# A pass over all tokens ahead of the mixer: LayerNorm, the dt path and the split of h move out of its half-steps, the decay masks become one fp32 operand, and TensorE takes a chunk's exponents at the end of a half-step

## The reference

```python
h = layernorm(x) * (1 + scale) + shift            # per batch b
zxbcdt = h @ W_in                                  # z 512, xBC 768, dt 8 heads
dt = softplus(dt + dt_bias);  A = -exp(A_log)
xBC = silu(conv4(xBC) + conv_b)                    # causal, 4 taps, per channel
h_t = h_{t-1} * exp(dt*A) + dt * x_t (x) B_t;  y_t = C_t . h_t + D*x_t
y = rms(y * silu(z)) @ W_out;  y = y + h
y = y + a * sigmoid(gate);  (a, gate) = y @ glu_w + glu_b
x2 = x + sign/size gate * layernorm(y)
out = x2 + gate * experts(layernorm(x2))           # 16 experts, top 4, and a shared one
```

## Time and profile before

| | us |
|---|---|
| median of 3 runs (2523.81 to 2525.84) | 2524.52 |
| the profiled execution | 2520.89 |
| its span | 2518.0 |
| first matmul of the mixer's xbc projection | 61.12 |
| first and last `add_h` (32 of them) | 115.0, 1267.6 |
| first load of the expert stage | 1285.7 |
| busy: PE, DVE, ACT, POOL | 2236.5, 1914.6, 1199.9, 854.9 |
| DMA queue of SP, share of its 16 engines | 7.5% |

### The profile page before, as it was taken

How to read it: one execution, slowest core, us unless ns; L and a number is a source line. 1 busy time by engine, 2 the same in 40 slices (tenths; PEclk the granted TensorE clock), 3 DMA queues, 4 the chain that set the end, 5 groups by cost and what they waited for, 6 DMA issues and landing times. The chain is left out here.

```text
span 2518.0 us, 43347 instructions
## 1 busy us (share of the span) xinstructions
PE 2236.5 (89%) x13488; PEld 1939.3 (77%) x13488; DVE 1914.6 (76%) x4376; ACT 1199.9 (48%) x2443; POOL 854.9 (34%) x729
## 2 busy tenths in 40 slices
PE   2788888888888888888759999999999999999998
PEld 2677777777777777777648888888888888888887
DVE  3799998899998899898847666766666665666755
ACT  1666766766766666676624333323333323333322
POOL 0233333333333333233323333333333333333333
PEclk7899999999999999999969999999999999999999
DMA  2000000000000000000031000000000000000000
GB/s 93 5 26 17 21 25 25 12 25 25 12 25 25 12 25 25 12 25 21 14 97 49 26 26 27 26 18 9 26 27 26 27 17 10 26 26 27 18 18 9
DMA packets 36586, 63.36 MB, mean 25 GB/s; under 512 B 4320, under 2 KB 13024, under 8 KB 36320
## 3 DMA queue, kind: packets, MB, share of 16 engines
q1 hardware_dynamic: 36448, 61.59, 7.5%
HBM read 44.80 MB, written 16.78 MB: 24 GB/s over the span
## 5 line engine op out<-in xcount | busy, mean ns | idle before, releaser
L1673 POOL TENSOR_TENSOR fl<-ff,fh 128x512 fp32r<-128x512 f32 x272 | 353.0, 1298 | 761.2 <-ACT fh L1467 761.2
L1586 DVE TENSOR_TENSOR ff<-gs,bank 128x512 f32<-128x512 f32 x272 | 186.8, 687 | 380.0 <-ACT gs L1461 326.3
L104 PE MATMUL bank<-mhh,wh 128*128 128x512 f32 x1088 | 435.9, 401 | 9.7 <-issue 9.7
L105 PE MATMUL bank<-mhl,wh 128*128 128x512 f32 x1088 | 431.0, 396 | 0.0
L106 PE MATMUL bank<-mhh,wl 128*128 128x512 f32 x1088 | 430.4, 396 | 0.0
L1608 DVE SCALAR_TENSOR_TENSOR acc<-bank,comb,acc 128x256 f32<-128x256 f32 x960 | 398.0, 477 | 8.9
L1467 ACT ACTIVATE fh<-ff 128x512 fp32r<-128x512 f32 x272 | 172.1, 633 | 447.4 <-DVE ff L1586 414.1
L1461 ACT ACTIVATE gs<-bank 128x512 f32<-128x512 f32 x272 | 162.5, 598 | 368.4 <-PE bank L106 368.4
L875 DVE SCALAR_TENSOR_TENSOR cv<-xc,convw,cv 128x256 f32<-128x256 f32 x576 | 321.2, 624 | 1.9 <-ACT cv L701 1.9
L104 PE MATMUL bank<-wh,fh 128*128 128x256 f32 x1088 | 306.9, 282 | 3.6 <-issue 1.6
L106 PE MATMUL bank<-wh,fl 128*128 128x256 f32 x1088 | 305.6, 281 | 0.0
(11 more groups left out here) (185 smaller groups left out, 5009.4 us busy)
## 6 DMA issues: line engine op xcount, KB each, us to landing
xt<-in_x SPq DMA_DIRECT2D x32, 256.0 KB, 2.7
xr<-in_x SPq DMA_DIRECT2D x32, 256.0 KB, 2.6
x_dram<-xr SPq DMA_DIRECT2D x32, 256.0 KB, 2.0
x<-x_dram SPq DMA_DIRECT2D x16, 512.0 KB, 3.6
xres<-x_dram SPq DMA_DIRECT2D x16, 512.0 KB, 4.5
out<-yo SPq DMA_DIRECT2D x16, 512.0 KB, 3.2
raw<-in_experts SPq DMA_DIRECT2D x17, 384.0 KB, 3.2
wmod<-in_wmod SPq DMA_DIRECT2D x1, 1536.0 KB, 6.4
```

Of the source, the lines that this page charges most:

```text
L104: pe.matmul(out, a_hi, b_hi, start=start, stop=False, skip_group_check=True)
L105: pe.matmul(out, a_hi, b_lo, start=False, stop=False, skip_group_check=True)
L1586: dve.tensor_tensor(ff[e % 2][:, :], g, UP[e % 2][:, :], ALU.mult).then_inc(ff_done, 1)
L1673: pool.tensor_tensor(fl[e % 2][:, :], ff[e % 2][:, :], fh[e % 2][:, :].bitcast(F32), ALU.subtract).then_inc(fl_done, 1)
```

## The change

A new function `prepare_tokens` runs ahead of the mixer, over all 8192 tokens in 16 groups of 512. It loads x, takes mean and variance, applies them, transposes, modulates twice from PSUM (hT and hh), subtracts (hl), projects dt into one PSUM bank for all tokens, and stores hT, hh and hl to DRAM. Then softplus runs once on 128x512 values, the three sums follow, and five parameters for each token and head (dt, a, and three exponentials or products) go to DRAM as `par_dram`. The splits of the weights, which stood in a block of their own, run in the same pass. The mixer's half-steps load hTh, hTl, hT and the parameters (`load_halves`, `load_h`, `load_par`) and lose the work listed above.

The decay masks are one fp32 operand: `mask_a` on DVE writes it, and `exponents` multiplies it by the fp32 matrix `after` with one matmul for four heads where there were two fp32r ones. In PE's list `exponents` of chunk 0 moves to the end of the half-step before.

```diff
+    x = [sb(f"px{n}", [P, MT, D]) for n in range(XBUF)]        # XBUF = 4
+    hT = two("phT", ...); hh = two("phh", ..., F32R); hl = two("phl", ..., F32R)
+        def load(n):
+            if n >= XBUF:
+                sp.wait_ge(xnT_ps, KD * (n - XBUF + 1))
+            sp.dma_start(x[n % XBUF]..., rows(t["x"], n)...)
+        def store(n):
+            for done, dst, src in ((hT_done, h_dram[0], hT), (hh_done, h_dram[1], hh), (hl_done, h_dram[2], hl)):
+                sp.wait_ge(done, ...)
+                sp.dma_start(rows(dst, n).rearrange("s p k t -> p k s t"), src[n % 2]...).then_inc(stored[n % 2], 16)
...
+        def modulate(n):
+            if n >= 2:
+                act.wait_ge(stored[n % 2], 48 * (n // 2))
...
+        pe.wait_ge(c_in, CONSTS)
+        turn(0)
+        for n in range(GROUPS):
+            if n + 1 < GROUPS:
+                turn(n + 1)
+            project_dt(n)
+        pe.wait_ge(a_done, 1)
+        for n, m in enumerate((upto, after, ones)):
+            pe.matmul(SUMS[n][:, :], m[:, :], a[:, :], start=True, stop=True).then_inc(sums_ps, 1)
...
 def exponents(b, i, c):
-    pe.wait_ge(au_done[b], CH * i + c + 1)
-    pe.wait_ge(lo_done[b], CH * i + c + 1)
+    pe.wait_ge(mask_done[b], CH * i + c + 1)
     if c == 0:
         pe.wait_ge(xc_done[b], 3 * i + 3)
         pe.wait_ge(tap0_done[b], 3 * i + 3)
-        pe.wait_ge(ex_done[b], i + 1)
+        pe.wait_ge(st_done[b], CH * i)
...
-        pe.matmul(Q(b, 2 + half_heads)[:, :], after_r[:, :], masked_hi[b]..., start=True, stop=False)
-        last = pe.matmul(Q(b, 2 + half_heads)[:, :], after_r[:, :], masked_lo[b]..., start=False, stop=True)
+        last = pe.matmul(Q(b, 2 + half_heads)[:, :], after[:, :], masked[b]..., start=True, stop=True)
...
 # PE's half-step
     if tail:
         project_out(*tail)
     if second:
-        exponents(*second, 0)
-    if first:
-        transpose_xn(*first)
-    if second:
         x_by_token(*second, 0)
         x_by_token(*second, 1)
     if tail:
         state_add(*tail, 1)
         glu(*tail)
-    if first:
-        project_dt(*first)
     if second:
         exponents(*second, 1)
...
     if first:
         project_z(*first, 0)
-        sums(*first)
     if second:
         transpose_y(*second, 1)
+    if first:
+        exponents(*first, 0)
...
 # DVE's half-step
+    if second:
+        mask_a(*second, 1)
     if tail:
         add_h(*tail)
...
-        mask_a_lo(*first, 0)
+        mask_a(*first, 0)
```

More of the change, by code:

```diff
@@ L203, in mixer @@
+def mixer(nc, sem, prime, t, mod, gate_ln, ident, minus_half, bank, h_dram, par_dram, x2_dram):
     with ExitStack() as ctx:
@@ L253, in mixer @@
         btok = both("btok", [P, CH, NS])
[L254 to L257, removed]
+        masked = both("masked", [P, CH, H, P])
         dec = both("dec", [P, CH, H, P])
@@ L456, in half @@
                     if more:
-                        load_x(*following(second))
+                        load_halves(*following(second))
+                    if first:
+                        load_par(*first)
+                        load_h(*first)
                     if tail:
@@ L511, in project_z @@
                     last.then_inc(z_ps[b], 1)
-                def sums(b, i):
-                    pe.wait_ge(a_done[b], i + 1)
-                    a = dts[b][:, 7, :, :]
-                    for n, m in enumerate((upto, after, ones)):
-                        last = pe.matmul(Q(b, 3)[:, 64 + n * CH * H:64 + (n + 1) * CH * H], m[:, :],
-                                         a.rearrange("p c h -> p (c h)"), start=True, stop=True)
-                    last.then_inc(sums_ps[b], 1)
                 def x_by_token(b, i, c):
@@ L552, in exponents @@
                         heads = slice(half_heads * 4, half_heads * 4 + 4)
-                        pe.matmul(Q(b, 2 + half_heads)[:, :], after_r[:, :],
-                                  masked_hi[b][:, c, heads, :].rearrange("p h i -> p (h i)"), start=True, stop=False)
-                        last = pe.matmul(Q(b, 2 + half_heads)[:, :], after_r[:, :],
-                                         masked_lo[b][:, heads, :].rearrange("p h i -> p (h i)"),
-                                         start=False, stop=True)
+                        last = pe.matmul(Q(b, 2 + half_heads)[:, :], after[:, :],
+                                         masked[b][:, c, heads, :].rearrange("p h i -> p (h i)"),
+                                         start=True, stop=True)
                     last.then_inc(dec_ps[b], 1)
@@ L1055, in half @@
                     if second:
-                        mask_a_lo(*second, 1)
-                    if more:
-                        norm1(*following(second))
-                    if second:
                         for c in range(CH):
@@ L1062, in half @@
                             times_end(*second, c)
-                    if first:
-                        softplus_head(*first)
                     if tail:
                         gated(*tail)
-                    if first:
-                        for step in range(5):
-                            softplus_step(*first, step)
                     if second:
@@ L1101, in half @@
                         mean_square(*second, 1)
-                    if first:
-                        for step in range(11, DT_LINKS):
-                            softplus_step(*first, step)
-                    if second:
                         split_yT(*second, 0)
                     if first:
-                        split_a(*first)
-                        mask_a_lo(*first, 0)
+                        mask_a(*first, 0)
                     if second:
                         split_yT(*second, 1)
-                    if more:
-                        apply1(*following(second))
                     if first:
                         conv(*first, 1)
-                for b in range(NB):
-                    norm1(b, 1)
-                    apply1(b, 1)
                 halves(dve, half)
@@ L1182, in half @@
                         split_y1(*tail)
-                    if first:
-                        split_h(*first)
                     if second:
@@ L1193, in half @@
                         root_y(*second, 1)
-                    if more:
-                        root_norm1(*following(second))
-                for b in range(NB):
-                    root_norm1(b, 1)
                 halves(pool, half)
```

533 lines of the change are left out of this document (281 added, 252 removed).

## The result

The median went from 2524.16 us to 2595.1 us: a ratio of 1.0281 [1.0263, 1.0299], slower by 71 us. The forecast was 2608, with 2555 to 2660 around it. The profiled execution took 2593.5 us.

What follows compares the result with a forecast made beforehand. The mixer was taken as bound by a chain through all engines, with waits and low clock on PE. First pass +119, first half-steps -7, half-steps -28: +84 us, a median of 2608, range 2555 to 2660.

Steps and rivals of the forecast that it cites:

- The pass: Ahead of the mixer: 16 groups at 6.5 us plus an uncovered tail, first xbc matmul at 180, +119 us.
- P: The mixer's half-step, from one add_h to the next: 37.18 us before, forecast 36.3, a gain of 28 us over 31.
- The row of waits in the half-step: PE's half-step walked from o, the end of project_out: waits of 1.7 us before the GLU, 1.9 before chunk-0 exponents.
- The half-step's low clock: PE in the mixer: a low stretch of 1.5 us in some three of four half-steps, +1.1 us on each half-step.
- the walk without it: Mixer half-step on PE at full clock, from one end of project_out to the next: 35.2 us.
- the engines need less: In the first pass: PE 5.3 us a group, below the 6.5 us of loads and stores.
- the 302 of the earlier trace: First pass's stores: 1 KB runs go at 302 GB/s with DMA engines full, 5.2 us a group.
- The rival in which the pass overlaps at full rate: First pass: 1 KB stores at 416 GB/s, so engines' 5.4 us a group decide; -22 us, 2586; chance 0.13.
- The prologue: First half-steps, with no norm, dt and mask chain ahead of them: 7 us shorter.
- DVE as the bound: Mixer: DVE sets the period, half-step 29.7 us, -120 us in all, 2405; chance 0.11.
- the decision point named for that rival: Mixer half-step below 33.6 us, where DVE setting the period would be decided.
- The rival in which the clock falls more often: Mixer: a further 1.5 us low stretch in each half-step, 37.5 to 37.8 us, total 2645; chance 0.16.

Runs made afterwards that it cites:

- experiment 3: Kernel before with fp32 masks written by DVE, and the next chunk 0's exponents at the end of the half-step: 2605.54 us, 1.0331 to the kernel before.
- experiment 1: Changed kernel with only the exponents of chunk 0 put back behind project_out: 2481.0 us, 0.9823 to the kernel before.
- experiments 2: Kernel before with the fp32 masks on DVE and one fp32 matmul for four heads, all else as before: 2423.94 us, 0.9603.
- experiment 4: Kernel before with the fp32 masks, plus sixteen ACT activations a half-step into a tile nobody reads: 2511.86 us, 0.9956 to the kernel before.
- experiment 9: Changed kernel without the h_t store and with POOL's root of group n+2 ahead of the subtraction of group n: 2580.75 us, 1.0237.

## Why the prediction held, and where it was off

**The direction and the mechanism were right.** The pass costs more than the half-steps give back. By the experiments, one edit on top of the other, from the kernel before: the masks alone -101 us (P -3.07), the moved work on top of them +57 (+129 for the pass, P -2.20, which is -68), the exponents at the end +114 (P +3.62). Each price holds where it stands in that row: put straight on the masks, the exponents at the end cost 182 us (experiment 3), and the moved work on top of both gives some 10 back. The row of waits in the half-step was met nearly to the tenth: the GLU at o + 3.4 behind 1.49 us of waiting (walked 3.4 and 1.7), chunk 1's exponents at 7.57 (7.65), `from_state` at 12.67 (12.75), pair 1 of xbc at 20.7 (20.85), the second transpose of y at 26.5 (26.85), the chunk-0 exponents at 28.95 behind 1.80 (29.15 and 1.9), released by `start_conv` as named.

**The number is nearer than its terms.** The half-steps gave 23 us more than forecast and the first matmul came 10.5 later; that 84 us of span were forecast and 73.7 measured is in part luck, as the two misses went opposite ways.

**The half-step's low clock was mis-sized.** P came out at 35.53 for 36.3. The term was +1.1 for a low stretch of 1.5 us in three of four half-steps; the walk without it gave 35.2. From one `add_h` to the next the trace has two lengths and nothing between: of 26 half-steps read from it 15 take 34.8 to 34.9 us and 11 take 36.5 to 36.6, those in which the chunk-0 exponents stand at 2.8 to 3.6 us instead of 1.96. So the stretch costs about what I gave it (1.65 us for 1.5), but comes in two of five half-steps and not in three of four: 0.42 x 1.65 = 0.7, and the walk was 0.3 to 0.4 long elsewhere. The half-steps gave 51 us instead of 28.

**The pass was mis-sized the other way, by a term that stood at nothing.** It shifted the first matmul by 129.5 us, not 119. The groups took 7.2 us each instead of 6.5, +10.6 (the prediction named 6.8 with the landing and summed with 6.5). The step that failed is "the engines need less": it adds up PE's transposes and dt matmuls, POOL's subtraction and DVE's own work, and leaves out the splits of the weights, which run in the same pass. In the four groups that carry one, 11.1 us for 6.5 each, they added 18.4 us; the other eleven took 5.8 and gave 7.8 back. For these eleven the DMA engines were near full, as forecast, at a share of 0.95 behind the splits, but moved 325 GB/s of loads and stores together, above the 302 of the earlier trace rows; and with a third of the stores gone they come to 5.2, near PE's 5.01 at half clock, for which the prediction had 5.3. So the sum of each engine's work was right, and what it lacked is the wait that a weight split puts into two hand-written lists. The rival in which the pass overlaps at full rate, at 5.4 us a group, left out the same term. The splits' part is read from the trace and was not tried by itself.

Around the groups the misses nearly cancel: the start at 39.5 was met; from the last group's first modulation to softplus it took 7.4 us where 3.5 was put down; from 155.03 to 176.80 it is 21.8 where 21.1 to 21.6 was walked, softplus 15.6 as forecast, with a reciprocal of 3.35; and from the store of the parameters to the first matmul 13.8 for 15.7.

The Trainium skill (DMA: Bandwidth & Descriptors, Specifications) gives 512 bytes as the smallest transfer for line rate; runs of 1 and 2 KB differed here by 0.03 in share at 287 and 295 GB/s between 45 and 140 us, so nothing in these runs decides between its rule and the earlier trace rows, and the time did not hang on it.

**The prologue** gave 6.1 us for 7.

**The rivals.** DVE as the bound is out: its share fell from 0.92 to 0.75 and P by 1.65. Yet the decision point named for that rival, P below 33.6, is passed in experiment 1 with 31.91, by another cause: the order. The rival in which the clock falls more often wanted P at 37.5 and a low stretch in every half-step; P was 35.53, and the stretch came in two of five. What the prediction did not ask is what each part is worth by itself. It booked the masks as a wash, since PE's work stayed the same within half a microsecond; in truth they are the largest gain of the three, because they take sixteen small activations from ACT ahead of the decays that PE waits for, and PE's clock stays up behind the shorter waits (experiments 2 and 4), and the order, which the walk had right in its place, hid that gain: a wait of 1.9 us for one of 1.81 looked even, while with the masks alone that 1.81 is down to 0.39.

**What stays open.** The order costs 5.6 us a half-step with norm and dt still inside (experiments 2 and 3) and 3.6 without (experiment 1 and the changed kernel). The waits are of one size, 3.1 and 2.9; the difference is the clock, low in nearly every half-step of the one and in two of five of the other, where every second or third half-step is a long one. Why it stays up in three of five half-steps whose instructions and waits are the same was not tried by itself. Nor was a pass with the splits of the weights in a block of their own, or with ACT's high part ahead of the modulation.

## What to carry to other kernels

When a change bundles several edits, price each one against the kernel without the others: two of this change's three parts gain 3.1 and 2.2 us in each half-step, and the third, one block moved in a hand-written order, takes 3.6 back. A mean over groups of a stage can hide that some of them do something else: look at the distance from one to the next before naming what bounds them. A block of matmuls belongs where its engine waits anyway, and its output bank must be long free there; which of the waits behind it takes it in shows only in the trace; ask of each new place which engine frees the bank last. Work hoisted out of a loop of overlapping engines has to pay for itself at its full, uncovered length: here 129 us of pass bought 68 us of half-steps.

## What the runs showed of the hardware

- TensorE's granted clock was 0.50 (1.2 GHz) through the whole pass, 45 to 145 us, although PE was busy 71.54 of 100 us, with 128-column transposes and 8-column dt matmuls; in experiment 9 it was busy without a gap for 30 us, from 106 to 136, and the clock was 0.50 still. The Trainium skill (TensorE: Matmul & The Clock Gate, Part 4: PE-mode transpose) says that transpose mode does not count as busy in the same way as other matmuls; the row agrees, but no run took the transposes out, nor the small matmuls, so which of the two goes with the low clock stays open.
- In the mixer the clock fell behind two waits close together (0.84 and 1.80 us) in some half-steps and not in others of the same order, and each half-step took 34.9 or 36.5 us by that.
- A RECIPROCAL of 128x512 on VectorE took 3.35 us, a tensor_tensor of that size 0.69: 4.9 times as long.
- Two fp32 matmuls of 512 columns take 1.72 us at full clock (712.35 to 714.07 in experiment 1), 0.86 each, where one fp32r matmul takes 0.23: 3.7 times, so that two fp32r ones are the cheaper form on PE; here they cost ACT sixteen small activations a half-step and DVE the split of a.
- A DVE operation beside a POOL subtraction can last until that ends: the apply of 128x256 took 408 ns in the median and 2523 at most, four of them 1.38 us without POOL beside them and 3.49 with it. It goes the other way too: the same POOL subtraction of 128x512 took 1.56 us in the median in the changed kernel and 2.72 in experiment 1, both times beside DVE's conv; what decides which of the two is held up was not tried.
- ACT's small operations are dear for their size: 388 ns for 128x128 in experiment 4, against 595 for an exponential of 128x512, four times as many elements, there.
- DMA queues busy at a share of 0.95 moved 325 GB/s of loads and stores together (the changed kernel, 109 to 147 us).
